# Two hidden-layer products moved, two pieces of an attention product joined, and a shorter spacing of a block inverse in a PE-bound two-layer kernel

## The chip, the cores and the metric

The kernel runs on one core of a Trainium2 chip. TensorE (PE) multiplies, VectorE (DVE) and ScalarE (ACT) move and transform what it leaves in PSUM, GpSimd (POOL) does small elementwise work, and SyncE (SP) issues DMAs. Every engine works through its own list of instructions in order, and semaphores tie the lists together. The metric is the device time of one launch in microseconds, the median of three runs.

## The reference, cut to what matters

Input is `x` of shape (8, 512, 128): eight sequences of 512 tokens. Two layers follow each other, and each multiplies an attention-like term by a gate.

```python
xn = _layernorm(x, axis=-1)
s = _L0_attn_ref(xn, ...)                 # causal softmax attention, 16 heads of 8
g = _silu(_L0_ffn_ref(xn, ...))           # 8 experts, top 2: gelu(x w1 + b1) w2 + b2, weighted by gates
x = x + s * g
xn = _layernorm(x, axis=-1)
s = _L1_attn_ref(xn, ...)                 # h = layernorm; W -= 0.01 * (W k - v) k^T token by token; y = W q
g = _silu(_L1_ffn_ref(xn, weight))        # x @ sign(weight).T
x = x + s * g
```

The expert layer's hidden product is `h = gelu(einsum('bsd,edh->bseh', x, w1) + b1)`. The recurrence of the second layer is computed in four chunks of 128 tokens; each needs the inverse of a unit triangular 128x128 matrix.

## The kernel before, in words

Eight sequences pass through a pipeline. One call of `iteration` is a **round**. In a round four sequences are in work: `second` gets its query and key stacks, `nxt` has its row maxima taken, `cur` its attention, and `prev` its second layer. A full round runs over four groups (0 to 3) of ten units (0 to 9). A unit on TensorE is `s_unit` of `nxt` (L944, L947, read by one VectorE reduction, L1480) and `e_unit` of `cur` (L917, L921, L925, read by one ScalarE exponential, L1265). Each has two PSUM banks, so `s_unit` number u waits for the reduction of u-2 and `e_unit` for the exponential of u-2.

All other work is cut into pieces. The table `PLAN` puts them behind a unit: `(2, 8): ["lev_a5", "k"]` means that behind unit 8 of group 2 come the pieces lev_a5 and k. **Every engine walks the same table**, and runs its own part of a piece at that place of its list. A piece's place thus fixes both when TensorE multiplies and behind which reductions and exponentials VectorE and ScalarE serve it. Group 4 is only the tail of a round: no units, the pieces alone. The pieces the text speaks of:

- `h0` to `h3` (TensorE L865, ScalarE L1244 with the bias): the hidden product of `nxt`, one 128x512 product each into the one bank `ps_a`; `gelu` (L1248) follows on ScalarE, and needs another activation table, as the exponential behind it does again. `gb0` to `gb3` (L872, VectorE L1464) multiply `cur`'s hidden values by the gates; `out` (L879, L881) is the second product, followed by tanh (L1252, ScalarE) and L1469 (VectorE).
- `pv0`, `pv1`, `pv2` (L963): probabilities times values of a group, in three pieces. `yT` is the copy of its bank (L1271 on ScalarE or L1493 on VectorE), `yt` (L973) the transposition behind it, then L1504 and L1507 on VectorE; at the end of a round `x1` (L671, L675 on GpSimd) makes the input of the second layer, whose statistics are L1392 and L1397.
- `lev_a1` to `lev_a6`, `lev_d1` to `lev_d6`: levels of the inverse. Up to level 4 both are 16 products of 32x32 tiles (L1028). ScalarE copies what `lev_a` leaves (L1305), VectorE subtracts what `lev_d` leaves (L1543) and transposes (L1526). The next `lev_a` waits for the subtraction. `low_blocks` (L1564, two VectorE copies) and `turned0`, `turned1` (L1316, two ScalarE copies each) put the squares where `lev_a6` (L1054) reads them; it waits for both.
- `c_u`, `c_y`, `c_r` (L1112; L1122 and L1124; L1101 and L1103): the scan over the four chunks. `c_y` waits for ScalarE's copy of what `c_u` left (L1327), the next `c_u` for VectorE's L1576.
- `xnt`, `q`, `k` (L817, L829) of `second`; ScalarE's cast (L1217) and VectorE's subtraction (L1416) empty the bank behind q and k. `vl0`, `vl1` (L844), `m_rows0`, `m_rows1` (L888, copied by ScalarE L1257) use `ps_a` as well: whoever fills this bank waits until its last user is through.

Of the kernel before, what the change touches and what calls it, by code (L numbers as in the profile page):

```python
# [18 lines left out]
ALU = mybir.AluOpType  # L19
# [5 lines left out]
P = 128  # L25
# [71 lines left out]
PLAN_SECOND = ("load_x", "ln1_stats", "ln1_rstd", "ln1_norm", "xnt", "q", "k", "stacks0", "stacks1")  # L97
PLAN_NEXT = ("rn", "vl0", "vl1", "route", "v_out", "logits", "gates", "gate_norm", "gt", "h0", "h1", "h2", "h3", "gelu", "v", "m_parts0", "m_rows0", "m_parts1")
PLAN_OLDER = ("c_u3", "c_y3", "c_out")
PLAN_CURRENT = ("gb0", "gb1", "gb2", "gb3", "out", "pv0", "pv1", "pv2", "yt", "x1", "m_rows1", "zero_state")  # L100
SEQUENCES = 8


# [39 lines left out]
def iteration(second, nxt, cur, prev, older, plan=PLAN):  # L143

    for step in range(1 + max(at[0] for at in plan)):
        for u in range(UNITS):
            if step < GROUPS:
                yield "unit", (cur, nxt, step, u)
            for name in plan.get((step, u), []):
                if name.startswith("fill"):  # L150
                    yield "fill", (int(name.removeprefix("fill")),)
                    continue
                if name in PLAN_COMMON:
                    yield name, ()
                    continue
                of = second if name in PLAN_SECOND else nxt if name in PLAN_NEXT else \
                    cur if name in PLAN_CURRENT or name.startswith("last:") else older if name in PLAN_OLDER else prev
                name = name.removeprefix("last:").removeprefix("prev:")
                if of is not None:
                    yield name, (of, step) if name in ("pv0", "pv1") else (of, step - 1) if name in ("pv2", "yt") else (of,)  # L160


def schedule():
# [33 lines left out]
def two_layers(nc, x_in, W_dq, W_uq, W_dkv, W_uk, W_uv, W_o, w1_in, b1_in, w2_in, b2_in, cent_in, route_in,  # L197
# [8 lines left out]
    with ExitStack() as ctx:  # L206
        def sb(name, shape, dt=F32):
            return ctx.enter_context(nc.sbuf_tensor(name, shape, dt))
# [518 lines left out]
        def _(pe):  # L727
# [81 lines left out]
            def tok(i):  # L809
                return slice(i * P, (i + 1) * P)  # L810
# [63 lines left out]
            def out_piece(b):  # L874
                a_fill(b, "out")
                pe.wait_ge(S["b2_ready"], PARTS)
                for i in range(NT):
                    for c in range(NC):
                        mm(ps_a[:, tok(i)], hid[:, c, tok(i)], w2s[:, c, :], start=(i == 0 and c == 0), stop=False,  # L879
                           skip_group_check=True)  # L880
                    last = mm(ps_a[:, tok(i)], gT[:, tok(i)], b2s[:, :], start=False, stop=True, skip_group_check=True)  # L881
                last.then_inc(S["a_filled"], 1)

            def m_rows(b, half):
                a_fill(b, f"m_rows{half}")
# [64 lines left out]
                last.then_inc(S["s_filled"], 1)  # L950


            def pv(b, grp, piece):

                if piece == 0:
                    after(pe, S["v_emptied"], b.count(2 * FILLS, 2 * (grp // FILLS)))
                    if grp == 0:
                        pe.wait_ge(S["v_ready"], b.count(FILLS, FILLS))
                pe.wait_ge(S["e_emptied"], b.count(GROUPS * UNITS, UNITS * grp + (4, 8, 10)[piece]))
                for j, u0, at in (((0, 0, 0),), ((1, 4, 0), (3, 4, 384)), ((2, 8, 0),))[piece]:  # L960
                    for hh in range(GH):
                        u, o = (u0 + hh, at) if j != 2 else (u0 + hh // 2, 256 * (hh % 2))
                        last = mm(ps_v[32 * hh:32 * hh + 32, P * j:TOK], vaug[:, j, head_of(grp, hh), :],  # L963
                                  prob[:, u, o:o + TOK - P * j], start=(j == 0 and grp % FILLS == 0),
                                  stop=(j == 2 and grp % FILLS == FILLS - 1), skip_group_check=True)
                last.then_inc(S["pv_used"], 1)

            def yt(b, grp):
                if grp % FILLS < FILLS - 1:
# [145 lines left out]
            def c_y(b, c):  # L1115
# [11 lines left out]
                elif c == NT - 1 - (b.c == SEQS - 1):  # L1127
                    last.then_inc(r.S["c1_filled"], 1)

            pieces = {"xnt": xnt, "q": lambda b: qk(b, 0), "k": lambda b: qk(b, 1), "v": v, "logits": logits, "vl0": lambda b: values_and_logits(b, 0), "vl1": lambda b: values_and_logits(b, 1), "gt": gt,  # L1130
                      "out": out_piece, "m_rows0": lambda b: m_rows(b, 0), "m_rows1": lambda b: m_rows(b, 1), "pv0": lambda b, grp: pv(b, grp, 0), "pv1": lambda b, grp: pv(b, grp, 1), "pv2": lambda b, grp: pv(b, grp, 2), "yt": yt, "c_xn2t": c_xn2t, "c_ht": c_ht, "c_kt": c_kt,
                      "c_qt": c_qt, "c_vk": c_vk, "c_gram": c_gram, "c_ffn": c_ffn}
            for c in range(NC):
                pieces[f"h{c}"] = lambda b, c=c: h(b, c)
# [13 lines left out]
        def _(act):  # L1148
# [92 lines left out]
            def h(b, c):  # L1241
                a_full(b, f"h{c}")
                after(act, S["gelu_ready"], b.count(1, 0))
                af(hid[:, c, :], ps_a[:, :], ACT.Identity, bias=vecT[:, c:c + 1]).then_inc(S["a_emptied"], 1)  # L1244

            def gelu(b):
                act.wait_ge(S["a_emptied"], A_NUMBER[b.c, "h3"] + 1)
                af(hid[:, :, :], hid[:, :, :], ACT.Gelu).then_inc(S["gelu_ready"], 1)  # L1248

            def out_piece(b):  # L1250
                a_full(b, "out")
# [72 lines left out]
            def c_u(b, c):  # L1324
# [3 lines left out]

            pieces = {"xnt": xnt, "q": lambda b: split_hi(b, 0), "k": lambda b: split_hi(b, 1), "v": v, "gates": gates, "gt": gt,
                      "vl0": lambda b: values_and_logits(b, 0), "vl1": lambda b: values_and_logits(b, 1),  # L1330
                      "gelu": gelu, "out": out_piece, "m_rows0": lambda b: m_rows(b, 0), "m_rows1": lambda b: m_rows(b, 1), "pv2": pv, "c_xn2t": c_xn2t, "c_ht": c_ht, "c_kt": c_kt,
                      "c_qt": c_qt, "c_gram": c_gram, "c_ffn": c_ffn}
            for c in range(NC):
                pieces[f"h{c}"] = lambda b, c=c: h(b, c)
# [9 lines left out]
        def _(dve):  # L1344
# [258 lines left out]
            def c_y(b, c):  # L1603
# [9 lines left out]
                else:  # L1613
# [52 lines left out]
```

## Time and profile before

| | |
|---|---|
| median of 3 runs | 616.99 us (615.72 to 617.30) |
| the profiled execution, device time | 615.89 us |
| its span | 614.2 us |
| PE busy | 576.2 us, 94% |
| DVE busy | 391.7 us, 64% |
| ACT busy | 352.7 us, 57% |
| POOL busy | 176.8 us, 29% |
| chain that ended last | PE 80%, DVE 10%, ACT 4% |

Full rounds with four sequences in work start near 185.5, 252.6, 321.2 and 389.9 us in the span; the one from 457.0 us has no `second` any more, and the two from 60.5 and 114.8 us lack the older sequences. All seven use `PLAN`. The last round from 523.0 us has a table of its own, which stays as it is. A time in a row is us from the span's start; PEclk is the granted TensorE clock as a share of full speed.

### The profile page before, as it was taken

The numbers are of one execution on the slowest core, as the hardware profiler recorded it, in microseconds if no ns is written. First come the engines' busy times: TensorE is split into PE (matmuls) and PEld (weight loads), VectorE is DVE, ScalarE is ACT, GpSimd is POOL, SyncE is SP. The second block draws the span as 40 slices with busy tenths as digits, with TensorE's granted clock in tenths as the row PEclk, the third lists the DMA queues.
The fourth block names the chain that finished last, engine by engine and source line by source line (L and its number), as shares of the span: only waits on it lengthen the run. The fifth ranks groups of instructions, "written<-read, shape, count | busy, mean of one in ns | idle before, by whom it ended". The sixth has DMA issues, their size and how long they took to land.

```text
span 614.2 us, 17394 instructions
## 1 busy us (share of the span) xinstructions
PE 576.2 (94%) x7233; PEld 385.2 (63%) x7233; DVE 391.7 (64%) x975; ACT 352.7 (57%) x678; POOL 176.8 (29%) x351
## 2 busy tenths in 40 slices
PE   7789999898998999899998999899998999799897
PEld 3345565476665876677665876678665776555465
DVE  4478775765757776767757676867667675511553
ACT  4421656763666566765666466765675576666231
POOL 7157122411304312431214221532224200311221
PEclk9899999998999999999998999999998999999999
DMA  4766193847134105510253105510262000000001
GB/s 117 151 157 136 25 98 83 160 66 69 53 91 94 45 11 109 120 43 3 62 110 67 44 12 124 103 45 3 72 122 49 22 12 1 26 18 2 3 4 34
DMA packets 58161, 39.41 MB, mean 64 GB/s; under 512 B 17956, under 2 KB 57987, under 8 KB 58083
## 3 DMA queue, kind: packets, MB, share of 16 engines
q1 hardware_dynamic: 58051, 38.29, 31.0%
q8 instruction: 57, 0.93, 0.7%
q14 instruction: 21, 0.17, 0.1%
q10 hardware_dynamic: 32, 0.01, 0.0%
HBM read 24.46 MB, written 9.96 MB: 56 GB/s over the span
## 4 chain that ended last, share of the span: by engine, by line
PE 80%; DVE 10%; ACT 4%; issue 2%; DMA 1%; POOL 1%; SPq 0%; DVEq 0%; POOLq 0%
PE ps_v L963 13%; PE ps_s L944 12%; PE ps_e L925 6%; PE ps_a L879 5%; PE ps_c L1028 4%; PE ps_a L865 4%; PE ps_e L917 3%; PE ps_e L921 3%; DVE cand L1480 3%; PE ps_a L829 3%; PE ps_s L947 3%; PE ps_e L747 3%; PE ps_c L1112 2%; PE ps_c L1010 1%; PE ps_a L844 1%
## 5 line engine op out<-in xcount | busy, mean ns | idle before, releaser
L1480 DVE TENSOR_REDUCE cand<-ps_s 128x4 f32<-128x512 f32 (+1 forms) x320 | 213.5, 686 | 75.9 <-PE ps_s L947 47.5
L1265 ACT ACTIVATE prob<-ps_e 128x512 f32<-128x512 f32 x320 | 187.8, 598 | 88.7 <-PE ps_e L925 52.6
L944 PE MATMUL ps_s<-kst,qst 72*128 72x128 bf16 (+2 forms) x1024 | 126.3, 236 | 15.0 <-DVE cand L1480 11.2
L944 PEld LDWEIGHTS ps_s<-kst,qst 72*128 72x128 bf16 (+1 forms) x1024 | 73.0, 98 | 79.7 <-DVE cand L1480 40.8
L925 PE MATMUL ps_e<-qst,kst 75*128 75x256 bf16 (+3 forms) x416 | 105.4, 284 | 0.0
L963 PE MATMUL ps_v<-prob,vaug 128*32 128x512 f32 (+3 forms) x1024 | 89.5, 451 | 0.0
L917 PE MATMUL ps_e<-identb,negmask 128*128 128x150 bf16 (+3 forms) x320 | 73.2, 229 | 3.2 <-ACT prob L1265 3.0
L921 PE MATMUL ps_e<-qst,kst 128*128 128x128 bf16 x384 | 75.1, 221 | 0.0
L925 PEld LDWEIGHTS ps_e<-qst,kst 75*128 75x128 bf16 x416 | 40.9, 98 | 3.5
L747 PE MATMUL ps_e<-identb 128*128 128x512 bf16 x115 | 40.0, 402 | 1.9 <-POOL identb L521 1.9
L921 PEld LDWEIGHTS ps_e<-qst,kst 128*128 128x128 bf16 x384 | 38.2, 100 | 4.5 <-issue 0.3
L947 PE MATMUL ps_s<-negmask,identb 128*128 128x300 bf16 (+1 forms) x128 | 41.0, 320 | 0.0
L963 PEld LDWEIGHTS ps_v<-prob,vaug 128*32 128x32 f32 x1024 | 24.0, 109 | 25.8 <-issue 20.0
L917 PEld LDWEIGHTS ps_e<-identb,negmask 128*128 128x128 bf16 x320 | 31.4, 98 | 13.9 <-ACT prob L1265 9.4
L1028 PEld LDWEIGHTS ps_c<-second 32*32 32x32 f32 x2072 | 25.2, 107 | 23.3 <-issue 18.2
L650 POOL CAST mparts<-nm 128x32 bf16<-128x32 f32 x16 | 3.3, 209 | 120.7 <-DVE nm L1487 120.7
L1028 PE MATMUL ps_c<-second 32*32 32x32 f32 x2072 | 33.0, 194 | 4.2 <-issue 1.8
L865 PE MATMUL ps_a<-xnT,w1s 128*128 128x512 f32 x64 | 33.6, 605 | 1.3 <-ACT hid L1244 0.8
L879 PE MATMUL ps_a<-w2s,hid 128*128 128x128 f32 x256 | 33.3, 283 | 0.7 <-ACT mrow L1257 0.7
L879 PEld LDWEIGHTS ps_a<-w2s,hid 128*128 128x128 f32 x256 | 31.1, 192 | 1.6 <-ACT mrow L1257 1.0
L1244 ACT ACTIVATE hid<-ps_a,vecT 128x512 f32<-128x512 f32 x32 | 22.0, 687 | 17.1 <-PE ps_a L865 17.1
L696 POOL TENSOR_TENSOR second<-second,second_flat 128x512 f32<-128x512 f32 x7 | 8.9, 1266 | 57.2 <-ACT second_flat L1286 43.4
(344 smaller groups left out, 924.7 us busy)
## 6 DMA issues: line engine op xcount, KB each, us to landing
qst<-q_scratch SPq DMA_DIRECT2D x48, 192.0 KB
kst<-k_scratch SPq DMA_DIRECT2D x48, 192.0 KB
q_scratch<-qparts SPq DMA_DIRECT2D x24, 128.0 KB, 2.3
k_scratch<-kparts SPq DMA_DIRECT2D x24, 128.0 KB, 2.3
x_res<-in_L_attn_x_dram SPq DMA_DIRECT2D x8, 256.0 KB, 4.3
xn<-in_L_attn_x_dram SPq DMA_DIRECT2D x7, 256.0 KB, 3.3
out_dram<-second SPq DMA_DIRECT2D x7, 256.0 KB, 2.5
max_scratch<-mrow SPq DMA_DIRECT2D x16, 96.0 KB, 1.9
```

Of the source, the lines that this page charges most:

```text
L747: mm(ps_e[:, 1, :].rearrange("p (a c) -> p a c", c=P), identb[:, :], bcast(identb[:, :], 1, 4), start=True, stop=True, skip_group_check=True)
L865: mm(ps_a[:, :], w1s[:, 2 * c:2 * c + 2, :].rearrange("p e f -> p (e f)"), xnT[b.parity][:, :], start=True, stop=True)\
L879: mm(ps_a[:, tok(i)], hid[:, c, tok(i)], w2s[:, c, :], start=(i == 0 and c == 0), stop=False, skip_group_check=True)
L917: mm(diag, negmask[:, :], bcast(identb[:, masked:P], 1, len(todo)), start=True, stop=False, skip_group_check=True)
L921: last = mm(ps_e[:, bank, at:at + P], k[:, hd, tok(j)], q[:, hd, tok(j)], start=False, stop=True, skip_group_check=True)
L925: last = mm(ps_e[:, bank, at + own:at + TOK - P * j], k[0:SROWS, hd, tok(j)], q[0:SROWS, hd, P * j + own:TOK], start=False, stop=True, ski ...
L944: last = mm(ps_s[:, bank, w * n:w * (n + 1)], q[0:rows, hd, tok(i)], k[0:rows, hd, keys[0]:keys[1]], start=(n == 0), stop=True, skip_group ...
L947: last = mm(ps_s[:, bank, :].rearrange("p (a c) -> p a c", a=GH)[:, :, masked:P], identb[:, :], bcast(negmask[:, masked:P], 1, GH), start= ...
L963: last = mm(ps_v[32 * hh:32 * hh + 32, P * j:TOK], vaug[:, j, head_of(grp, hh), :], prob[:, u, o:o + TOK - P * j], start=(j == 0 and grp % ...
L1028: last = mm(bank[SQ * col:SQ * col + SQ, SQ * i:SQ * i + SQ], lhsT(row, col, i), rhs[SQ * row:SQ * row + SQ, i, :], start=True, stop=True, ...
L1265: af(prob[:, u, :], ps_e[:, u % 2, :], ACT.Exp).then_inc(S["e_emptied"], 1)
L1480: vec.tensor_reduce(cand[:, i, h0:h0 + FILLS * (len(hds) - 1) + 1:FILLS, S_SLOT[u]], ps_s[:, u % 2, :].rearrange("p (a c) -> p a c", a=len ...
```

## The change

Six things change in the kernel; the arithmetic is the same.

- `h0` and `h1` of `nxt` stand in group 0 behind units 2 and 4, not in group 3. Since `gb` of `cur` still reads its hidden values, `hid` becomes two buffers by parity. `gb0`, `gb1`, `gb2` move back: behind unit 8 of group 0 and units 1 and 2 of group 1.
- `pv1` and `pv2` are one piece `pv12`, at the place of `pv2` (behind unit 2 of the next group).
- The levels stand closer: `lev_a1` stays behind (1, 5), then one step behind nearly each unit; `lev_d6` is at (2, 9) and not at (3, 2).
- `turned0`, `turned1`, `low_blocks` stand at (2, 3), (2, 5), (2, 7) and not at (2, 7), (2, 9), (3, 0).
- The scan fills group 3: `c_u0` at (3, 0), `c_y0` (3, 1), `c_r1` (3, 2) and so on.
- At the end of a round `c_y2` stands ahead of `pv12`, and `c_r3` ahead of `yt`.

```diff
-    (0, 0): ["c_u3"], (0, 1): ["gb0"], (0, 2): ["ln2_stats", "c_y3"], (0, 4): ["ln2_rstd", "hn_norm"],
-    (0, 6): ["pv0"], (0, 7): ["c_ht", "rn", "c_out"], (0, 8): ["gb1"], (0, 9): ["pv1", "c_kt", "c_qt"],
...
-    (2, 9): ["pv1", "lev_d5", "turned1"], (3, 0): ["stacks0", "h0", "low_blocks"], (3, 1): ["lev_a6"], (3, 2): ["h1", "lev_d6", "pv2"], (3, 3): ["c_u0"],
...
+    (0, 0): ["c_u3"], (0, 2): ["ln2_stats", "c_y3", "h0"], (0, 4): ["h1", "ln2_rstd", "hn_norm"],
...
+    (2, 7): ["low_blocks"], (2, 8): ["lev_a6", "k"], (2, 9): ["lev_d6"], (3, 0): ["stacks0", "h2", "c_u0"], (3, 1): ["c_y0"],
...
-        hid = sb("hid", [P, NC, TOK])
+        hid = [sb(f"hid{p}", [P, NC, TOK]) for p in range(2)]
...
-            def pv(b, grp, piece):
+            def pv(b, grp, pieces):
...
-                pe.wait_ge(S["e_emptied"], b.count(GROUPS * UNITS, UNITS * grp + (4, 8, 10)[piece]))
-                for j, u0, at in (((0, 0, 0),), ((1, 4, 0), (3, 4, 384)), ((2, 8, 0),))[piece]:
+                pe.wait_ge(S["e_emptied"], b.count(GROUPS * UNITS, UNITS * grp + (4, 8, 10)[pieces[-1]]))
+                for j, u0, at in [tile for n in pieces for tile in (((0, 0, 0),), ((1, 4, 0), (3, 4, 384)), ((2, 8, 0),))[n]]:
...
-                last.then_inc(S["pv_used"], 1)
+                last.then_inc(S["pv_used"], len(pieces))
...
-                af(hid[:, c, :], ps_a[:, :], ACT.Identity, bias=vecT[:, c:c + 1]).then_inc(S["a_emptied"], 1)
+                af(hid[b.parity][:, c, :], ps_a[:, :], ACT.Identity, bias=vecT[:, c:c + 1]).then_inc(S["a_emptied"], 1)
```

On TensorE at the end of a round and into group 0, before (L872 is gb0, L1124 is c_y3):

```order
L973 MATMUL ps_v<-ident,yT 128x128 x4
L1101 MATMUL ps_c<-state,second_flat 128x128
L1103 MATMUL ps_c<-state,second_flat 128x128
L944 MATMUL ps_s<-kst,qst 128x128 x4
...
L872 MATMUL ps_a<-gT,pick 128x512
L944 MATMUL ps_s<-kst,qst 128x128 x4
...
L1124 MATMUL ps_c<-u_sb,second 128x128
L944 MATMUL ps_s<-kst,qst 128x128 x4
```

and now:

```order
L1101 MATMUL ps_c<-state,second_flat 128x128
L1103 MATMUL ps_c<-state,second_flat 128x128
L973 MATMUL ps_v<-ident,yT 128x128 x4
L944 MATMUL ps_s<-kst,qst 128x128 x4
...
L1124 MATMUL ps_c<-u_sb,second 128x128
L865 MATMUL ps_a<-xnT,w1s 128x512
L944 MATMUL ps_s<-kst,qst 128x128 x4
```

gb0 has left this place, h0 (and behind unit 4 h1) has come in, and the scan's product c_r3 has moved ahead of the transposition.

On VectorE in the second half of group 2, before (xn<-ps_a is q's subtraction, krest<-ps_a that of k):

```order
L1480 TENSOR_REDUCE cand<-ps_s 128x2 x2
L1416 TENSOR_TENSOR xn<-ps_a,qparts 128x512
L1543 TENSOR_TENSOR second<-second,ps_c 128x128
L1526 STREAM_TRANSPOSE second<-second 128x128
L1480 TENSOR_REDUCE cand<-ps_s 128x2 x2
L1416 TENSOR_TENSOR krest<-ps_a,kparts 128x512
```

and now (L1564 is low_blocks):

```order
L1480 TENSOR_REDUCE cand<-ps_s 128x2
L1416 TENSOR_TENSOR xn<-ps_a,qparts 128x512
L1480 TENSOR_REDUCE cand<-ps_s 128x2
L1564 COPY second<-second 32x4x32 x2
L1480 TENSOR_REDUCE cand<-ps_s 128x2
L1416 TENSOR_TENSOR krest<-ps_a,kparts 128x512
```

The two copies that lev_a6 waits for now stand behind q's subtraction and one reduction. On TensorE the same place reads, now (L829 w_q is q, L1054 lev_a6):

```order
L829 MATMUL ps_a<-xnT,w_q 128x512
L944 MATMUL ps_s<-kst,qst 128x256 x2
...
L944 MATMUL ps_s<-kst,qst 128x256 x2
...
L1054 MATMUL ps_c<-second 64x64 x4
L829 MATMUL ps_a<-xnT,w_k 128x512
```

Only two units lie between q and lev_a6.

## Rows read from the trace of the kernel before

**Rows 1.** Two full rounds: stretch, length, busy PE PEld DVE ACT POOL, PEclk, DMA, GB/s
```profile
252.60:321.20 68.60, 66.59 (x900) 46.86 (x898) 47.91 (x121) 43.17 (x83) 20.02 (x36) 0.98 0.29 63
389.90:457.00 67.10, 65.10 (x900) 46.43 (x898) 47.78 (x121) 43.14 (x83) 20.00 (x36) 1.00 0.29 65
```
**Rows 2.** The same view, where the clock is down, and ahead of it
```profile
255.57:258.98 3.41, 1.73 (x23) 1.28 (x23) 3.38 (x13) 1.80 (x4) 1.65 (x4) 1.00 0.91 179
258.98:262.39 3.41, 3.41 (x20) 1.20 (x18) 2.39 (x7) 1.19 (x2) 2.51 (x4) 0.50 0.17 41
463.78:467.19 3.41, 3.41 (x19) 1.26 (x18) 2.08 (x7) 1.16 (x2) 2.21 (x3) 0.50 0.04 9
```
**Rows 3.** Timeline from yt to unit 5: start, us, engine, line [idle before <-releaser]
```profile
388.92 0.66 PE L973 MATMUL ps_v<-ident,yT 128*128 128x128 f32 x4 [0.17 <-DVE yT L1493]
391.86 1.27 POOL L675 TENSOR_TENSOR x<-x_res,att 128x512 f32<-128x512 f32 x1
393.37 0.86 DVE L1392 BATCH_NORM_STATS2 stats<-x 128x6 f32<-128x128 f32 x4
395.13 1.28 DVE L1480 TENSOR_REDUCE cand<-ps_s 128x4 f32<-128x512 f32 x2
395.88 0.39 PE L944 MATMUL ps_s<-kst,qst 72*128 72x256 bf16 x2 [1.68 <-DVE cand L1480]
```
**Rows 4.** Timeline of TensorE: pv1, pv2, and both in one
```profile
341.54 0.64 PE L963 MATMUL ps_v<-prob,vaug 128*32 128x256 f32 x8
342.11 0.40 PE L944 MATMUL ps_s<-kst,qst 128*128 128x128 bf16 x4
...
370.05 1.07 PE L963 MATMUL ps_v<-prob,vaug 128*32 128x384 f32 x16
371.05 0.59 PE L1028 MATMUL ps_c<-second 32*32 32x32 f32 x24
...
386.61 1.50 PE L963 MATMUL ps_v<-prob,vaug 128*32 128x384 f32 x24
388.04 0.49 PE L1122 MATMUL ps_c<-u_sb,vk 128*128 128x128 f32 x2
```
**Rows 5.** Timeline around q, and the two copies of low_blocks later
```profile
366.44 0.45 PE L1028 MATMUL ps_c<-second 32*32 32x32 f32 x32
366.82 0.39 PE L944 MATMUL ps_s<-kst,qst 72*128 72x256 bf16 x2
367.16 0.69 DVE L1416 TENSOR_TENSOR xn<-ps_a,qparts 128x512 f32<-128x512 f32 x1 [1.90 <-ACT qparts L1217]
367.35 0.38 PE L944 MATMUL ps_s<-kst,qst 72*128 72x256 bf16 x2
368.32 1.25 DVE L1480 TENSOR_REDUCE cand<-ps_s 128x2 f32<-128x512 f32 x2
373.22 0.45 DVE L1564 COPY second<-second 32x128 f32<-32x128 f32 x2
```
**Rows 6.** Timeline behind h0
```profile
372.20 1.02 PE L865 MATMUL ps_a<-xnT,w1s 128*128 128x512 f32 x2
373.06 0.38 PE L944 MATMUL ps_s<-kst,qst 128*128 128x128 bf16 x4
373.26 0.69 ACT L1244 ACTIVATE hid<-ps_a,vecT 128x512 f32<-128x512 f32 x1 [0.27 <-PE ps_a L865]
```
**Rows 7.** Timeline behind out
```profile
352.50 0.38 PE L944 MATMUL ps_s<-kst,qst 72*128 72x256 bf16 x2
353.33 0.69 DVE L1469 SCALAR_TENSOR_TENSOR gate_out<-tG,ps_a 128x512 f32<-128x512 f32 x1 [3.16 <-ACT tG L1252]
```
**Rows 8.** Groups of ACT by line: busy us, mean ns of one | idle before
```profile
L1257 ACT COPY mrow<-ps_a 96x512 bf16<-96x512 bf16 x16 | 9.2, 577 | 2.4 <-PE ps_a L888 1.9
L1316 ACT COPY second<-second 32x128 f32<-32x128 f32 x28 | 8.2, 294 | 1.9 <-DVE second L1526 1.4
L1327 ACT COPY u_sb<-ps_c 128x128 f32<-128x128 f32 x28 | 7.3, 262 | 7.9 <-PE ps_c L1112 7.7
```

More of the change, by code:

```diff
@@ L60 @@
 PLAN = {
[9 rows of a table removed]
+    (0, 0): ["c_u3"], (0, 2): ["ln2_stats", "c_y3", "h0"], (0, 4): ["h1", "ln2_rstd", "hn_norm"],
+    (0, 6): ["pv0"], (0, 7): ["c_ht", "rn", "c_out"], (0, 8): ["gb0"], (0, 9): ["c_kt", "c_qt"],
[7 rows of a table added]
 }
@@ L99 @@
 PLAN_OLDER = ("c_u3", "c_y3", "c_out")
-PLAN_CURRENT = ("gb0", "gb1", "gb2", "gb3", "out", "pv0", "pv1", "pv2", "yt", "x1", "m_rows1", "zero_state")
+PLAN_CURRENT = ("gb0", "gb1", "gb2", "gb3", "out", "pv0", "pv1", "pv2", "pv12", "yt", "x1", "m_rows1", "zero_state")
 SEQUENCES = 8
@@ L159, in iteration @@
                 if of is not None:
-                    yield name, (of, step) if name in ("pv0", "pv1") else (of, step - 1) if name in ("pv2", "yt") else (of,)
+                    yield name, (of, step) if name in ("pv0", "pv1") else (of, step - 1) if name in ("pv2", "pv12", "yt") else (of,)
 def schedule():
@@ L878, in out_piece @@
                     for c in range(NC):
-                        mm(ps_a[:, tok(i)], hid[:, c, tok(i)], w2s[:, c, :], start=(i == 0 and c == 0), stop=False,
+                        mm(ps_a[:, tok(i)], hid[b.parity][:, c, tok(i)], w2s[:, c, :], start=(i == 0 and c == 0), stop=False,
                            skip_group_check=True)
@@ L950, in s_unit @@
                 last.then_inc(S["s_filled"], 1)
-            def pv(b, grp, piece):
-                if piece == 0:
+            def pv(b, grp, pieces):
+                if 0 in pieces:
                     after(pe, S["v_emptied"], b.count(2 * FILLS, 2 * (grp // FILLS)))
@@ L1130, in _ @@
             pieces = {"xnt": xnt, "q": lambda b: qk(b, 0), "k": lambda b: qk(b, 1), "v": v, "logits": logits, "vl0": lambda b: values_and_logits(b, 0), "vl1": lambda b: values_and_logits(b, 1), "gt": gt,
-                      "out": out_piece, "m_rows0": lambda b: m_rows(b, 0), "m_rows1": lambda b: m_rows(b, 1), "pv0": lambda b, grp: pv(b, grp, 0), "pv1": lambda b, grp: pv(b, grp, 1), "pv2": lambda b, grp: pv(b, grp, 2), "yt": yt, "c_xn2t": c_xn2t, "c_ht": c_ht, "c_kt": c_kt,
+                      "out": out_piece, "m_rows0": lambda b: m_rows(b, 0), "m_rows1": lambda b: m_rows(b, 1), "pv0": lambda b, grp: pv(b, grp, (0,)), "pv1": lambda b, grp: pv(b, grp, (1,)), "pv2": lambda b, grp: pv(b, grp, (2,)), "pv12": lambda b, grp: pv(b, grp, (1, 2)), "yt": yt, "c_xn2t": c_xn2t, "c_ht": c_ht, "c_kt": c_kt,
                       "c_qt": c_qt, "c_vk": c_vk, "c_gram": c_gram, "c_ffn": c_ffn}
@@ L1243, in h @@
                 after(act, S["gelu_ready"], b.count(1, 0))
-                af(hid[:, c, :], ps_a[:, :], ACT.Identity, bias=vecT[:, c:c + 1]).then_inc(S["a_emptied"], 1)
+                af(hid[b.parity][:, c, :], ps_a[:, :], ACT.Identity, bias=vecT[:, c:c + 1]).then_inc(S["a_emptied"], 1)
             def gelu(b):
                 act.wait_ge(S["a_emptied"], A_NUMBER[b.c, "h3"] + 1)
-                af(hid[:, :, :], hid[:, :, :], ACT.Gelu).then_inc(S["gelu_ready"], 1)
+                af(hid[b.parity][:, :, :], hid[b.parity][:, :, :], ACT.Gelu).then_inc(S["gelu_ready"], 1)
             def out_piece(b):
@@ L1330, in _ @@
                       "vl0": lambda b: values_and_logits(b, 0), "vl1": lambda b: values_and_logits(b, 1),
-                      "gelu": gelu, "out": out_piece, "m_rows0": lambda b: m_rows(b, 0), "m_rows1": lambda b: m_rows(b, 1), "pv2": pv, "c_xn2t": c_xn2t, "c_ht": c_ht, "c_kt": c_kt,
+                      "gelu": gelu, "out": out_piece, "m_rows0": lambda b: m_rows(b, 0), "m_rows1": lambda b: m_rows(b, 1), "pv2": pv, "pv12": pv, "c_xn2t": c_xn2t, "c_ht": c_ht, "c_kt": c_kt,
                       "c_qt": c_qt, "c_gram": c_gram, "c_ffn": c_ffn}
@@ L1463, in gb @@
                 dve.wait_ge(S["gelu_ready"], b.count(1, 1))
-                vec.tensor_tensor(hid[:, c, :], hid[:, c, :], ps_a[:, :], ALU.mult).then_inc(S["a_emptied"], 1)
+                vec.tensor_tensor(hid[b.parity][:, c, :], hid[b.parity][:, c, :], ps_a[:, :], ALU.mult).then_inc(S["a_emptied"], 1)
             def out_piece(b):
@@ L1621, in _ @@
                       "q": lambda b: split_rest(b, 0), "k": lambda b: split_rest(b, 1), "logits": logits, "route": logits, "gates": gates, "gate_norm": gate_norm,
-                      "out": out_piece, "m_parts0": lambda b: m_parts(b, 0), "m_parts1": lambda b: m_parts(b, 1), "pv2": pv, "yt": yt, "c_vk": c_vk, "c_gram": c_gram, "c_ffn": c_ffn, "x1": x1_piece, "early_out": early_out}
+                      "out": out_piece, "m_parts0": lambda b: m_parts(b, 0), "m_parts1": lambda b: m_parts(b, 1), "pv2": pv, "pv12": pv, "yt": yt, "c_vk": c_vk, "c_gram": c_gram, "c_ffn": c_ffn, "x1": x1_piece, "early_out": early_out}
             for c in range(NC):
```

12 rows, old and new, of the table PLAN are left out of this document.

## The prediction

> **What bounds the kernel now.** I read the busy time by stretches first. A full round takes 67.1 us where the clock stays up, and PE is busy for 65.1 of them; VectorE reaches 47.8 and ScalarE 43.1 [rows 1]. So PE's list sets the time: every wait on PE counts in full, and work that moves along it counts only by the waits it fills or makes. Second, the timeline around each start of a round. PE stands for 1.68 us before the `s_unit` of unit 5 in group 0, for VectorE's reduction of unit 3 [rows 3]; so it does in each of five rounds. Third, the clock. One full round takes 68.6 us, not 67.1 [rows 1], with the same count of matmuls. In it the clock is at half (1.2 GHz) for 3.41 us, right behind a stretch in which PE was busy for 1.73 of 3.41 us, the one with the wait [rows 2]. Of the five rounds of [rows 3]'s kind three have this fall (first and last in [rows 2]), the two others not, with the same wait. A fall costs 68.6 - 67.1 = 1.5 us.
>
> **Part 1: h0, h1 in group 0.** What ends the 1.68 us wait is a chain that starts with yt at 388.92: two VectorE pieces, two GpSimd products (x1 ends at 391.86 + 1.27 = 393.13), the statistics from 393.37, a sum, and the reduction of unit 3 (the first of the two from 395.13, so to 395.77); PE goes on at 395.88 [rows 3]. That is 6.96 us from yt. In the new order VectorE has no gb0 in the way (0.69, as any pass over a 128x512 bank, L1469 in [rows 7]), but x1 is hardly earlier than VectorE came anyway (393.13 against 393.37), so the chain still takes 6.8. PE's own work over the same stretch was 6.96 less its waits: 1.68, 0.2 for the exponential behind the activation table, 0.2 for c_u3, so about 4.8. Now c_r3 (0.45) and gb0 (0.22) leave it and h0 and h1 come in, 373.06 - 372.20 = 0.86 each [rows 6]: 4.8 - 0.67 + 1.72 = 5.85. Waits fall from 2.1 to 0.95 us, split into two of half a microsecond. Gain 1.2 us a round. c_r3 gains nothing by itself: it fills the wait for yT that c_y2 filled (PE L973 still waited 0.17 there, [rows 3]).
>
> **Part 2: one piece for two.** pv1 takes 371.05 - 370.05 = 1.00 us of PE's list, pv2 342.11 - 341.54 = 0.57; both in one take 388.04 - 386.61 = 1.43 [rows 4]. So a join is worth 0.14. It happens in groups 0 to 2 (behind group 3 they already ran as one): 0.42 a round, and about 0.1 for one fewer change from wide products to 32-wide ones. 0.5.
>
> **Part 3: the spacing.** PE's work is the same; what counts is whether VectorE and ScalarE, which walk the same table, are through. A unit is 367.35 - 366.82 = 0.53 us of PE [rows 5], with the wider mask product of units 0 to 3 and some of the later ones 0.6.
> - `lev_a6` (largest). q ends at 366.3 (the next piece starts at 366.44); VectorE's subtraction for q runs 367.16 to 367.85, since ScalarE casts first [rows 5]. Behind it now stand one reduction (1.25 / 2 = 0.63) and the two copies of low_blocks (0.45) [rows 5]: 367.8 + 0.6 + 0.45 = 368.8. PE gets there two units behind q, at 366.3 + 0.53 + 0.6 = 367.5. Wait 1.3 us, where none of this kind was. Queued behind lev_a6 on PE are k, and through k the stacks of the next sequence; these had microseconds to spare.
> - `xnt`: waits for ScalarE's copy of m_rows0 (0.58), ahead of which turned0 (2 x 0.29) now stands [rows 8] and, with it, the copy of lev_a5. 0.4.
> - `vl0`: gb2 is one unit ahead of it, and VectorE's product is through 0.42 + 0.69 after gb2 starts (the pass is that of L1469, [rows 7]); PE arrives after 0.22 + 0.6. 0.3.
> - `lev_a3`: lev_d2's subtraction stands behind L1469, which ends at 354.02, 1.5 us after out [rows 7], and one reduction and itself (0.6 + 0.3); PE arrives 2.05 behind out. 0.3.
> - `c_y0`, `c_y1`: each is one unit behind c_u, whose copy (0.26, [rows 8]) stands behind h2's or h3's bias pass, which starts 0.2 after PE's next piece and takes 0.69 [rows 6]: ready after 1.13, PE arrives after 0.84 or 0.80. 0.6 for both.
> - `c_y2` 0.1 and `pv12` 0.3 at the end of a round: pv1 used to run there while the last exponential went on; pv12 needs that one first.
> - `lev_d1` 0.2, behind the transposition that follows gb3 on VectorE.
>
> Together 3.5 us a round. Three small waits of before go (c_y1, c_r1, lev_a5: 0.3). From both sides: the hand-over between engines reads as 0.1 to 0.2 us in these rows, so each of the nine waits may be 0.1 us off: 2.6 to 4.4 a round, 614.5 to 623.5 in the end. I take the middle, which the hand-over behind h0 (373.26 - 373.06 = 0.2, [rows 6]) and that of PE to VectorE's chain (395.88 - 395.77 = 0.1, [rows 3]) give.
>
> **Sum.** A full round: -1.2 - 0.5 - 0.3 + 3.5 = +1.5 us. Five rounds have all this: +7.5. In the round without `second` there is no q and no xnt, so 1.7 less: about 0. The first one has no inverse: joins and h0 against the later pv12, about 0. The clock: with no wait near 1.68 left at the round's start, the three falls go, -4.6. The new 1.3 us wait is shorter than those ahead of any fall, and I cost it no clock. Net +2.9 on 615.89. The median of the runs is 1.1 above that execution, less than one clock fall; since the new kernel has fewer places for falls I add only a little of it. **619.0 us.**
>
> **Rivals.**
> *Faster, 611 us (609 to 614).* The steps cost nothing much: VectorE and ScalarE catch up, and the waits of ScalarE's kind (xnt, c_y0, c_y1, pv12, 1.6 a round) vanish, which leaves 619 - 8 = 611. For it: ScalarE is busy for 43 of 67 us [rows 1]. Against: each wait above is a fixed chain behind PE's own product, not a matter of load.
> *Clock stays as it is, 623.6 us.* The fill is right but the falls have another cause, or the wait at lev_a6 takes them over: 619.0 + 4.6. For it: a fall came in only three of five rounds with the same wait [rows 2]. Against: in these five rounds it never came anywhere else. The Trainium skill (TensorE: Matmul & The Clock Gate, section "HAM oscillation") names as the cause idle gaps longer than any in these rounds; by it the 1.68 us wait costs no clock and this rival would hold. The trace disagrees as far as it goes, the clock being down right behind that wait.
> *No change, 617 us.* The lev_a6 wait is half of mine, as k, which waits on the same subtraction, loses its own wait in turn: 5 x 0.4 less.
> *Slower than all this:* if lev_a6 also held the clock down in every second round and each small wait were 0.1 longer, 625.
>
> **How the numbers follow.** What a measurement of this kernel can tell from no change is 0.3%, 1.85 us: faster is under 615.1, slower over 618.8. The forecast has 0.55 (own range 617 to 622), the faster rival 0.2, the kept clock 0.1, no change 0.15. Half of the forecast's chance and more lies above 618.8, with the kept clock 0.49; the faster rival and a bit make 0.21; 0.30 stays within. Range 612 to 623.5.
>
> **What the new profile would show.** The wait before L944 of unit 5 in group 0 near 0.5 us with L865 ahead of it, and PEclk at 1.00 in the full rounds. L963 in runs of 24 of 1.43 us. A wait of 1.3 us before L1054 on VectorE's L1564, the largest of the round; waits near 0.3 before L1122, before L817 on L1257, before L844 on L1464. Rounds of 68.6 us without a fall, against 67.1. I am wrong if rounds are under 67.1: then the wait at L1054 is missing or the chain behind yt is shorter than 6.8.

## The result: 3.1% slower, and the profile after

| | before | after |
|---|---|---|
| median of 4 runs each | 617.14 us (615.72 to 621.37) | 636.44 us (633.61 to 642.59) |
| the profiled execution, device time | 615.89 us | 638.92 us |
| its span, mean granted clock | 614.2 us, 0.986 | 637.2 us, 0.973 |

The ratio is 1.0314, with a 95% interval from 1.0252 to 1.0375. The forecast was 619.0 us (612 to 623.5): the direction was right, the size was not. Here and below the ratios are taken without the slow executions of a kernel (over 1.5% above its fastest, among them one of e5 of 1835.67 us and one of e6 of 900.86 us), while the medians are over all.

The same four rounds as around [rows 1], now with the changed kernel (stretch, length, busy PE PEld DVE ACT POOL, PEclk, DMA, GB/s):

```profile
192.20:266.30 74.10, 70.00 (x900) 49.84 (x899) 49.11 (x120) 43.07 (x83) 20.06 (x36) 0.93 0.25 58
266.30:339.50 73.20, 68.89 (x901) 48.69 (x900) 49.12 (x120) 43.11 (x83) 20.06 (x36) 0.95 0.25 60
339.50:409.40 69.90, 65.61 (x900) 46.80 (x898) 48.93 (x120) 42.92 (x83) 20.05 (x36) 1.00 0.27 63
409.40:481.00 71.60, 67.30 (x900) 47.74 (x899) 49.18 (x120) 43.09 (x83) 20.03 (x36) 0.98 0.27 61
```

One round has no clock fall: 69.9 us against 67.1, with the same number of matmuls and 0.5 us more of busy PE. The other 2.3 us of the 2.8 are waits. The other three rounds are 1.7, 3.3 and 4.2 us longer than that one, in step with their clock. VectorE is busy 1.1 us longer in a round, for the same work; that is the first sign of what follows.

Where PE waits (engine, line waited for, us in total, times, longest us):

```profile
PE ps_c L1054 <- issue: 12.3, 6, 2.4
PE ps_e L917 <- ACT prob L1265: 3.3, 6, 1.4
PE ps_s L944 <- DVE cand L1480: 3.3, 7, 1.1
PE ps_c L1028 <- issue: 2.9, 1, 2.9
PE ps_c L1028 <- DVE second L1543: 2.6, 6, 1.6
...
PE ps_c L1122 <- ACT u_sb L1327: 1.9, 10, 0.2
PE ps_v L973 <- DVE yT L1493: 1.9, 7, 0.8
```

The wait at `lev_a6` (L1054) is the largest: 2.4 us in each of five rounds (and 0.4 in a sixth), not the 1.3 forecast. It is listed under "issue", since the profile shows no releaser for it. The timeline in the clear round shows who was late (start, us, engine, line, [idle before <-releaser]):

```profile
386.77 0.69 DVE L1416 TENSOR_TENSOR xn<-ps_a,qparts 128x512 f32<-128x512 f32 x1 [1.81 <-ACT qparts L1217]
...
387.38 0.68 DVE L1480 TENSOR_REDUCE cand<-ps_s 128x2 f32<-128x512 f32 x1
387.53 0.61 POOL L616 CAST qparts<-xn 128x512 bf16<-128x512 f32 x1 [8.56 <-DVE xn L1416]
387.98 1.47 DVE L1564 COPY second<-second 32x128 f32<-32x128 f32 x2
388.22 1.15 POOL L618 TENSOR_TENSOR qparts<-xn,qparts 128x512 bf16<-128x512 f32 x1
...
389.55 0.65 PE L1054 MATMUL ps_c<-second 64*64 64x64 f32 x8 [2.40 <-issue]
```

The two copies of `low_blocks` (L1564) take 1.47 us, where [rows 5] has 0.45. They end at 389.45, and PE starts 0.1 later. GpSimd's second piece for q runs beside them, from 388.22 to 389.37 (L618; it is a subtraction, the expectations below call it a product). The durations of one copy, after and then before (ns min/median/max, first and last start):

```profile
L1564 DVE COPY second<-second x14: 203/234/1206, 167.6 to 608.3; 32x128 f32<-32x128 f32 x14
```
```profile
L1564 DVE COPY second<-second x14: 203/217/498, 168.6 to 585.2; 32x128 f32<-32x128 f32 x14
```

The second copy is the long one: 1205 or 1206 ns in all five rounds, where it takes 217 with GpSimd idle. It starts 0.03 us behind GpSimd's subtraction (1.15 us) and ends 0.08 behind that one's end. The first copy overlaps the end of GpSimd's cast (L616), ends 0.07 us behind it, and takes 233 to 235 ns, not 203 to 205. By this the copy is not slowed: it stands still until GpSimd is through. The Trainium skill (SBUF — State Buffer, section "SBUF: two separate sides") states this: VectorE in some of its modes and GpSimd share one pair of ports, and the pair "is an **exclusive lock**, not a bandwidth split"; who comes second waits for the whole instruction of the other. The trace agrees for this copy, with 1206 ns against 217.

This could be read in the trace of the kernel before. There the same subtraction stands at the very place where the copies were going to be put, and late in the span a copy already meets another GpSimd piece (L686):

```profile
367.92 0.61 POOL L616 CAST qparts<-xn 128x512 bf16<-128x512 f32 x1 [6.66 <-DVE xn L1416]
368.61 1.15 POOL L618 TENSOR_TENSOR qparts<-xn,qparts 128x512 bf16<-128x512 f32 x1
...
584.11 0.99 POOL L686 TENSOR_TENSOR qst<-qst,up_sq 128x384 f32<-128x384 f32 x1
584.67 0.75 DVE L1564 COPY second<-second 32x128 f32<-32x128 f32 x2
```

That pair takes 0.75 us and not 0.45; its first copy is the 498 ns above, and ends 0.07 us behind L686. Not all of VectorE's work is held so: the two reductions of [rows 5] from 368.32 (1.25 us for the two, as usual) run beside the subtraction from 368.61.

The clock, ahead of and behind this wait in the first and in the last of the three full rounds with a fall:

```profile
238.38:241.79 3.41, 1.52 (x15) 0.95 (x12) 2.23 (x4) 1.63 (x3) 1.43 (x2) 1.00 0.15 41
241.79:245.21 3.42, 2.90 (x11) 1.60 (x12) 1.11 (x2) 0.37 (x1) 0.33 (x1) 0.50 0.29 77
245.21:248.62 3.41, 3.41 (x27) 3.00 (x26) 2.08 (x4) 1.18 (x2) 1.74 (x2) 0.50 0.14 38
248.62:252.03 3.41, 3.41 (x15) 2.19 (x14) 0.80 (x2) 1.44 (x3) 0.02 (x1) 0.50 0.30 79
...
456.83:460.25 3.42, 1.02 (x15) 0.81 (x13) 3.26 (x5) 0.97 (x3) 1.76 (x2) 1.00 0.29 77
460.25:463.66 3.41, 3.41 (x17) 2.00 (x18) 0.92 (x2) 1.48 (x3) 0.17 (x1) 0.50 0.16 43
```

The clock is at half (1.2 GHz) for 10.2 us in the first of them (it falls 0.5 us before the wait ends there, and 0.5 to 1.0 us after its end in the others), 6.8 in the second and 3.4 in the last; in the round of the first inverse it is so for 6.8 us from 170.1, behind the wait that ends at 169.1. That is four of five. [Rows 2] showed the same at the start of a round, never for more than 3.4 us. These old falls are gone: no full round now falls at its start.

### The profile page after: what moved, and what is told of

The parts are those of the page before. It is cut to its first block, busy times and chain, and to the rows that moved or that the text cites. A ratio compares the mean times of both kernels' runs of the same rounds, so it can differ in the third digit from the quotient of the medians.

```text
span 637.2 us, 17394 instructions
## 1 busy us (share of the span) xinstructions
PE 586.7 (92%) x7233; PEld 393.8 (62%) x7233; DVE 398.1 (62%) x975; ACT 352.2 (55%) x678; POOL 177.1 (28%) x351
## 4 chain that ended last, share of the span: by engine, by line
PE 74%; DVE 7%; issue 7%; ACT 6%; POOL 4%; DMA 1%; SPq 0%; POOLq 0%; DVEq 0%
PE ps_v L963 12%; PE ps_s L944 11%; PE ps_e L925 6%; PE ps_a L879 5%; PE ps_c L1028 4%; PE ps_a L829 3%; PE ps_a L865 3%; PE ps_e L917 3%; PE ps_e L747 3%; PE ps_e L921 3%; PE ps_s L947 2%; PE ps_a L844 2%; PE ps_c L1122 2%; PE ps_c L1010 1%; DVE cand L1480 1%
## 5 line engine op out<-in xcount | busy, mean ns | idle before, releaser
L944 PEld LDWEIGHTS ps_s<-kst,qst 72*128 72x128 bf16 (+1 forms) x1024 | 75.9, 100 | 65.2 <-DVE cand L1480 29.7
L963 PE MATMUL ps_v<-prob,vaug 128*32 128x512 f32 (+3 forms) x1024 | 82.8, 439 | 0.7 <-ACT prob L1265 0.7
L1028 PEld LDWEIGHTS ps_c<-second 32*32 32x32 f32 x2072 | 25.3, 107 | 26.1 <-issue 18.4
L963 PEld LDWEIGHTS ps_v<-prob,vaug 128*32 128x32 f32 x1024 | 25.2, 109 | 24.8 <-issue 21.0
L1028 PE MATMUL ps_c<-second 32*32 32x32 f32 x2072 | 33.0, 194 | 6.5 <-issue 2.9
L865 PE MATMUL ps_a<-xnT,w1s 128*128 128x512 f32 x64 | 36.1, 648 | 1.4 <-ACT hid L1244 0.8
L1464 DVE TENSOR_TENSOR hid<-hid,ps_a 128x512 f32<-128x512 f32 x32 | 21.8, 681 | 10.1 <-PE ps_a L872 10.0
```

What stands on the lines that cost most here:

```text
L865: mm(ps_a[:, :], w1s[:, 2 * c:2 * c + 2, :].rearrange("p e f -> p (e f)"), xnT[b.parity][:, :], start=True, stop=True)\
L944: last = mm(ps_s[:, bank, w * n:w * (n + 1)], q[0:rows, hd, tok(i)], k[0:rows, hd, keys[0]:keys[1]], start=(n == 0), stop=True, skip_group ...
L1028: last = mm(bank[SQ * col:SQ * col + SQ, SQ * i:SQ * i + SQ], lhsT(row, col, i), rhs[SQ * row:SQ * row + SQ, i, :], start=True, stop=True, ...
```

## The experiments

Theory: the loss is the wait before `lev_a6`, and that wait has two parts that the forecast did not price, VectorE's copy standing behind GpSimd's subtraction (1.1 us) and the clock behind the wait. Rivals: GpSimd's piece is a bystander; the clock falls for some other reason; or the loss lies in the many small waits or in the two other parts of the change. Each table line below is one kernel. "Before" ran beside them on the same chip; its median was 617.14 for the result, 618.24 for e1 to e4, and 616.14 for e5 to e8, so between these three groups the ratio is what can be compared.

| kernel | median us | ratio to before [95%] |
|---|---|---|
| changed kernel | 636.44 | 1.031 [1.025, 1.038] |
| e1, copies before q | 613.38 | 0.996 [0.991, 1.000] |
| e2, GpSimd held back | 632.19 | 1.024 [1.017, 1.031] |
| e3, wait filled with products | 628.72 | 1.016 [1.011, 1.021] |
| e4, parts 1 and 2 without part 3 | 608.01 | 0.983 [0.979, 0.987] |
| e5, part 1 alone | 606.65 | 0.987 [0.983, 0.992] |
| e6, part 2 alone | 620.99 | 1.010 [1.006, 1.014] |
| e7, part 3 alone | 646.35 | 1.053 [1.045, 1.061] |
| e8, e4 with three waits filled | 601.11 | 0.979 [0.972, 0.986] |

**e1.** The changed kernel with one piece moved two units up:

```diff
-    (2, 5): ["xnt", "lev_d5", "turned1"], ... (2, 7): ["low_blocks"], (2, 8): ["lev_a6", "k"],
+    (2, 5): ["xnt", "lev_d5", "low_blocks", "turned1"], ... (2, 8): ["lev_a6", "k"],
```

> The changed kernel (profiled 638.9 us), with one piece moved: low_blocks, VectorE's two copies L1564, stands behind lev_d5 at (2, 5) and no longer behind q's subtraction at (2, 7). Theory 1 (lev_a6 waits for these copies, which stand late and collide there with GpSimd's product L618; the wait of 2.4 us brings the clock down): the wait before L1054 goes to under 0.2 us in all five full rounds, no clock falls near it, full rounds near 69.9 - 2.4 = 67.5 us; time 638.9 - 12.6 (falls) - 5 x 2.4 = 614, range 611 to 618. Rival (the profile puts the wait down to issue: PE's own instructions come late there): the wait before L1054 stays near 2.4 us and so does the time, 633 to 642.

Measured: 613.38 us, as expected, and 23 less than the changed kernel (22 by the ratios). The wait before L1054 is gone from the list of waits, the copies are back at 214/216/509 ns, and no full round has a clock fall. A full round is 67.6 us:

```profile
318.60:386.20 67.60, 65.71 (x901) 46.93 (x900) 47.90 (x120) 43.07 (x83) 20.05 (x36) 1.00 0.29 64
```

VectorE is at 47.90 us again. So the whole loss hangs on this one place: 69.9 - 67.6 = 2.3 us in each round, and the falls. The small waits of the new spacing are all still there and are not the cause of the loss. They do cost something: 67.6 us is 0.5 more than the clear round of before, though parts 1 and 2 are in.

**e2.** GpSimd's two pieces for q (cast and subtraction) now start behind the copies, the table is that of the changed kernel (the line numbers of its rows are two higher):

```diff
                 pool.wait_ge(S["a_emptied"], A_NUMBER[b.c, ("q", "k")[n]] + 1)
+                if n == 0 and b.c >= 3:
+                    pool.wait_ge(S["blocks_ready"], 2 * (b.c - 3) + 2)
```

> The changed kernel, order unchanged, but GpSimd's work on q (L616, L618) waits until VectorE's two copies L1564 are through. Theory 1 says that the second copy takes 1.2 us instead of 0.24 since it runs while GpSimd's L618 does: both copies then take 0.24, the wait before L1054 is 1.4 us as first forecast, and the clock falls less or not at all: full rounds near 68.9, time 619 to 623. Rival a (the copy is slow for another reason, such as its place or a VectorE wait): it stays at 1.2 us and the time at 633 to 642. Rival b (the port costs what I say, but a wait of 1.4 us still brings the clock down): time 624 to 632 with PEclk at 0.5 behind L1054.

Measured: 632.19 us. The same place of its timeline, and its largest waits:

```profile
377.90 0.45 DVE L1566 COPY second<-second 32x128 f32<-32x128 f32 x2
...
378.45 0.65 PE L1056 MATMUL ps_c<-second 64*64 64x64 f32 x8 [1.38 <-issue]
378.49 0.61 POOL L618 CAST qparts<-xn 128x512 bf16<-128x512 f32 x1 [9.59 <-DVE second L1566]
```
```profile
PE ps_c L1056 <- issue: 7.2, 6, 1.4
```

Nothing changed for VectorE but the moment at which GpSimd works, and the copies take 0.45 us again: GpSimd's subtraction was what held them. The wait is 1.4 us, the forecast's 1.3 within a tenth. The time, however, is not the 619 to 623 that I expected, but just above the 624 to 632 of rival b. It fell by 4.2 us, near the five times 1.0 that the waits give but not clear of the spread (the intervals of the two ratios overlap), and it is still 18.8 above e1. Of these, 7.2 are the waits. The clock is at half for 6.8 us behind two of them, at 379.7 and at 451.4; at 3.3 us each, as between the rounds of 73.2 and 69.9 above, that is 6.6. Another 3.4 come from falls at places that have nothing to do with this wait (one in the first round, and the one at 151.0, which lasts 6.8 us where e1 has 3.4). The remaining 1.6 are within the spread of its runs. So a wait of 1.4 us brought the clock down too, in two of five rounds, and the forecast would have been too low even with its own wait.

**e3.** The wait is as it was, but PE multiplies in it: ten 128x512 products into a free bank ahead of `lev_a6`, with results that nothing reads.

```diff
-    (2, 7): ["low_blocks"], (2, 8): ["lev_a6", "k"],
+    (2, 7): ["low_blocks"], (2, 8): ["warm", "lev_a6", "k"],
```

> The changed kernel, and ahead of lev_a6 TensorE runs ten extra 128x512 bf16 products (of the identity, into a bank that is free there; their result is overwritten). They take about 0.22 us each, 2.2 us, and fit into the wait. Theory 1: the wait for L1564 remains but PE is busy, so the clock stays up; full rounds 69.9 to 70.2 us, time 638.9 - 12.6 = 626, range 624 to 629. Rival (the clock falls for another reason, the order of the work behind q or the draw of this stretch): falls of 3.4 to 10 us remain behind L1054, time 633 to 642, or more by what does not fit.

Measured: 628.72 us, as expected. In its timeline the copies (L1571 there) still take 1.47 us, and PE's own wait is down to 0.24:

```profile
377.92 1.47 DVE L1571 COPY second<-second 32x128 f32<-32x128 f32 x2
...
379.49 0.65 PE L1054 MATMUL ps_c<-second 64*64 64x64 f32 x8 [0.24 <-issue]
```

Its clock is 0.992 against 0.973, with no fall in the full rounds behind `lev_a6`. The delay itself is unchanged: all four full rounds are 70.0 us, as long (within 0.1) as the clear one of the changed kernel. So 636.44 - 628.72 = 7.7 us is what the clock alone cost, in medians (9 by the ratios, whose intervals do not overlap). To e1 15.3 us are left. Of these, five times 2.4 = 12.0 are the stretch before `lev_a6`, now filled instead of empty; for the rest the trace has two falls elsewhere (3.4 us more at 147.7 than e1, and 3.4 at 540.2), 1.7 each. So the loss has two parts, some 8 to 9 us of clock and 12 of waiting, and no third of their size.

**e4.** The table of before with h0 and h1 in group 0, gb0 to gb2 moved back, and the joined pieces; levels, `turned`, `low_blocks`, the scan and the order at the end of a round as they were.

```diff
-    (2, 9): ["pv1", "lev_d5", "turned1"], (3, 0): ["stacks0", "h0", "low_blocks"], (3, 1): ["lev_a6"], (3, 2): ["h1", "lev_d6", "pv2"],
+    (2, 9): ["lev_d5", "turned1"], (3, 0): ["stacks0", "h2", "low_blocks"], (3, 1): ["lev_a6"], (3, 2): ["lev_d6", "pv12"],
```

> The changed kernel with the levels, turned0 and 1, low_blocks and the scan back at their places of before: h0 and h1 in group 0 with the two hidden buffers, and pv12, remain. My sum for these parts: -1.2 and -0.5 us a round, +0.3 for vl0 behind gb2, +0.3 for pv12 at the end of a round that must wait for the last exponential, and no clock falls at the start of a round (-4.6): 615.9 - 6 x 1.1 - 4.6 = 604.7, range 601 to 609. Rival (the h move or the joined piece themselves make the kernel slow): 616 or more.

Measured: 608.01 us, 1.7% under before. The start of a round has no fall any more. Its full rounds, however, are 67.2 us, no shorter than the clear ones of before, and its list of waits says why:

```profile
317.20:384.40 67.20, 65.01 (x901) 46.62 (x901) 48.09 (x121) 43.10 (x83) 20.09 (x36) 1.00 0.29 65
```
```profile
PE ps_c L1054 <- issue: 4.7, 5, 1.0
PE ps_v L963 <- ACT prob L1265: 3.2, 7, 0.7
```

pv1 used to stand between k and `lev_a6` and took 1.0 us. Without it PE gets to `lev_a6` that much earlier, and VectorE does not: the join turns work into a wait. At the end of a round the joined piece waits for the last exponential, which pv1 used to cover. I had put `lev_a6` into group 2 for the changed kernel, where this could not be seen. The 608.01 lies in the range that I gave (601 to 609), but not for my reasons: the 1.1 us a round did not come. The time came from the three old falls and from the round of the first inverse, 68.1 us here and 70.6 before, where a fall and a stall inside a level (L1028) are missing in this execution.

**e5.** e4 without the join: pv1 and pv2 apart, at the places of before.

> The order of before with h0 and h1 in group 0 and gb0 to gb2 moved back for them, and nothing else. Theory: the move takes most of the 1.68 us wait at the start of a round and with it the clock falls, and since pv1 stays between k and lev_a6 as before, the 1.0 us wait that the joined order has before lev_a6 does not arise, nor the 0.4 us at the end of a round. Full rounds 66.1 us where the joined one had 67.15: 602.5 us (600 to 605). Rival (my forecast's reading, by which a join is worth 0.5 us a round): without the joins 3 us more than with them, 611 us.

Measured: 606.65 us. A full round is 66.3 us, as expected, 0.9 less than in e4, and the waits before L1054 are gone:

```profile
318.10:384.40 66.30, 65.39 (x902) 46.50 (x900) 47.99 (x121) 43.00 (x83) 20.06 (x36) 1.00 0.28 65
```

The median is 4 us above what I expected. Its profiled execution gives back 3.4 us in the round from 114.0 (71.5 us, where e4 had 68.1), in which the first inverse is computed; the clock falls there twice. Which of e4 and e5 is faster as a whole the runs do not decide, since their ratios' intervals overlap. What is shown is the 0.9 us in the full rounds.

**e6 and e9.** The table of before with the joined pieces alone.

```diff
-    (0, 9): ["pv1", "c_kt", "c_qt"], ... (1, 2): ["c_gram", "pv2"],
+    (0, 9): ["c_kt", "c_qt"], ... (1, 2): ["c_gram", "pv12"],
```

> The order of before with pv1 and pv2 in one piece in all four groups, and nothing else. Theory: the piece itself saves 0.14 us three times, but its millisecond place matters more: without pv1 behind unit 9 of group 2, PE reaches lev_a6 1.0 us earlier and waits there for VectorE, and at the end of a round it waits 0.4 us for the last exponential. Full round +1.0 us, and the waits and falls at the round's start stay: 622 us (619 to 626). Rival (forecast): a join saves 0.5 us a round, 614 us.

> The kernel of e6 once more, for one profile, since the profiled execution of e6 ran at half the clock almost throughout. Theory: a wait of 1.0 us before lev_a6 (L1054) in five rounds, with the 1.68 us wait before L944 at the start of the rounds still there, and 0.5 us before the joined piece at the end of a round; clear rounds of 68.1 us. Rival: no wait at L1054 and clear rounds of 66.6 us.

Measured: 620.99 us, 1% slower than before: my forecast's reading (614) falls, and the theory's 622 stands. The profile is that of e9, one further execution of the same kernel, of 615.18 us. Its full round and its waits:

```profile
322.10:390.10 68.00, 64.59 (x901) 46.59 (x899) 47.91 (x121) 43.15 (x83) 20.10 (x36) 1.00 0.28 65
```
```profile
PE ps_s L944 <- DVE cand L1480: 11.2, 8, 1.7
PE ps_c L1054 <- issue: 4.7, 5, 0.9
PE ps_v L963 <- ACT prob L1265: 3.2, 7, 0.7
```

PE is busy for 0.5 us less than in [rows 1] and the round is 0.9 longer. Note also that the 1.7 us wait at the start of a round is there in each of them, and the clock stays up in the full ones. In this execution the wait of [rows 3] cost no clock at all in these rounds; in that of before it did in three of five. (One early round of e9 does have a fall, at 118.7, behind a wait of 1.48 us at the same place.)

**e7.** The changed kernel with everything but the spacing put back.

```diff
-    (0, 2): ["ln2_stats", "c_y3", "h0"], (0, 4): ["h1", "ln2_rstd", "hn_norm"],
+    (0, 1): ["gb0"], (0, 2): ["ln2_stats", "c_y3"], (0, 4): ["ln2_rstd", "hn_norm"],
```

> The changed kernel with its closer levels and scan, but with h0, h1, gb0 to gb2 and the pieces of probabilities times values at the places of before. Theory: it carries both kinds of clock falls, those at the round's start behind the 1.68 us wait and those behind lev_a6's 2.4 us wait, and is the slowest of all: 640 us (634 to 645). Rival (the parts of the change hurt together, not this one alone): 625 us or less.

Measured: 646.35 us, the slowest. Both waits stand in its list, and its clock is 0.966. As in the changed kernel, the clock falls at four of the five waits before `lev_a6`; at the five waits of 1.6 us at the round's start it falls twice:

```profile
PE ps_c L1054 <- issue: 12.3, 6, 2.4
PE ps_s L944 <- DVE cand L1480: 10.8, 9, 1.6
```

So part 3 by itself is worth +5.3%, and parts 1 and 2 together -1.7% (e4). Their sum, 3.6%, agrees with the 3.1% of all three within the intervals, so no large dependence shows between them. (The sixth item of the change, the order at the end of a round, is in neither e4 nor e7 and was not run alone.) I had expected 6 us less for e7; the trace shows two reasons, a longer wait for xnt's bank (L817, up to 0.6 us where 0.4 was forecast) and one stall of 4.8 us inside a level (L1028) in the round of the first inverse, 2.9 in the changed kernel's.

**e8.** e4 with its three waits filled by work that is there anyway: the joined piece of group 2 ahead of `lev_a6`, gb2 ahead of the joined piece of group 0, and pv1 and pv2 apart at the end of a round.

```diff
-    (1, 2): ["c_gram", "pv12", "gb2"], ... (3, 1): ["lev_a6"], (3, 2): ["lev_d6", "pv12"],
-    (3, 9): ["c_u2"], ... (4, 1): ["pv12", "c_y2"],
+    (1, 2): ["c_gram", "gb2", "pv12"], ... (3, 1): ["pv12", "lev_a6"], (3, 2): ["lev_d6"],
+    (3, 9): ["c_u2", "pv1"], ... (4, 1): ["pv2", "c_y2"],
```

> e4's order with three places mended: the joined piece of group 2 stands ahead of lev_a6 instead of behind lev_d6 (fills 0.95 us), gb2 ahead of the joined piece of group 0 instead of behind it (0.33 us), and at the end of a round pv1 and pv2 are apart as before (0.47 us). Theory: these are waits of PE in the clear and the clock stays up, so full rounds come to 65.4 us: 599.5 us (597 to 602). Rival: VectorE is the next limit there and takes the gain back as waits elsewhere, 604 us or more.

Measured: 601.11 us, as expected: 2.1% under before and, by the ratios, 5.1% under the changed kernel; the fastest here.

```profile
315.30:380.60 65.30, 64.64 (x902) 46.55 (x900) 48.10 (x121) 42.76 (x83) 20.05 (x36) 1.00 0.29 67
```

A full round has 0.7 us left in which PE is not busy; in [rows 1] it was 2.0. VectorE did not become the limit.

## Why the prediction was wrong, by its own steps

Lengths of a piece are taken from one start to the next on PE, in the clear round after (339.5 to 409.4) and before (389.9 to 457.0).

- **Part 1, h0 and h1: right.** Group 0 up to the end of unit 5 takes 6.85 us, before 6.61, though about 1.8 us of h0 and h1 came in and 0.22 of gb0 left: 1.3 us of waits gone, forecast 1.2. The wait at unit 5 is 0.38, with L865 ahead of it. The falls at the round's start are gone. In e5 it is worth 1.3% by itself.
- **Part 2, the join: right here.** L963 in runs of 24 takes 1.43 us, three times 0.14 less. At the round's end, c_y2, the joined piece and the waits cost 0.28 together, forecast 0.4. That the same join costs a round 0.9 us in the old spacing (e9) was outside my sum.
- **Part 3, the small waits: right.** Unit to unit: xnt 0.4 (forecast 0.4), vl0 0.4 (0.3), lev_a3 0.27 (0.3), c_y0 and c_y1 0.63 (0.6), lev_d1 0.16 (0.2).
- **Part 3, `lev_a6`: wrong in size.** The term was "the two copies of low_blocks (0.45)": they took 1.47 beside GpSimd's subtraction. From the start of the last unit ahead of lev_a6 to lev_a6 itself it is now 3.08 us, 2.40 of them the wait. I took the 0.45 from a row in which GpSimd was idle, and moved the copies to right behind the subtraction whose result GpSimd takes up 0.1 us later. The wait came out at 2.4 us where I had 1.3, in each of five rounds. The bounds of my own sum (2.6 to 4.4) did not hold it, because I gave every wait the same error of 0.1.
- **The clock: wrong.** "I cost it no clock." I argued from length: 1.3 was shorter than the 1.68 ahead of any fall. With 2.4 us the clock fell in four of five rounds, and with 1.4 (e2) in two of five.

The sum, in the profiled executions, is 638.92 - 615.89 = 23.0 us where I had +7.5 and -4.6. The clear round is +2.8, so 14.0 for the five rounds with the whole change, 6.5 more than forecast, of which 5.5 are `lev_a6`. The old falls went as forecast, -4.6. New falls at `lev_a6` cost 4.2 + 3.3 + 1.7 = 9.2 in the full rounds. The round of the first inverse is 5.8 longer than before, 2.8 of it as in a clear one; of the other 3.0, 1.1 are the stall inside a level (L1028 under "issue": 2.9 us, before 1.8), whose cause is open, and 1.9 are left for its new fall. That makes 11.1 for the clock, forecast 0. The round from 60.4 and the one from 481.0, forecast at about 0, add 1.0 and 0.7 (without its old fall). The sum is 14.0 + 11.1 + 1.1 - 4.6 + 1.7 = 23.3. So of the 20 us that I missed, 11 are clock and 5.5 the copies.

Of the rivals, the one with lev_a6 taking over the falls named the mechanism, but priced it at one 1.5 us fall for each old one; these falls last up to 10.2 us, not 3.4. (The faster rival's "1.6 a round" has a slip: its four terms, 0.4 + 0.6 for the two scan waits + 0.3, make 1.3.) The Trainium skill's rule that I weighed there (TensorE: Matmul & The Clock Gate, section "HAM oscillation") speaks of longer idle gaps than any in these rounds. The runs do not bear out that only those matter: filling the gap (e3) or removing it (e1) kept the clock up in the full rounds.

What stays open is when a given wait brings the clock down. The 1.68 us wait did so in three of five rounds before and in none of the full rounds of e9; the 2.4 us wait left one round untouched; 0.95 us never did in e4 or e9.

## What to carry to other kernels

Before you move a short VectorE copy that another engine waits for, look in the timeline at what GpSimd does at the new place, not the old one: a duration read where GpSimd is idle says nothing of it. Price a new wait on TensorE with the clock as well, from zero upwards: here, at `lev_a6`, waits of 0.95 us never brought a fall and waits of 1.4 us did in two of five rounds, and the falls behind the new wait were up to three times as long as any in the profile before. And when work is joined or saved, ask which wait it used to cover: here a join that took 0.14 us less each time cost a round 0.9 us where it stood behind the wait.

## What the runs showed of the hardware

A VectorE copy of 32x128 elements took 1206 ns instead of 217 when GpSimd's 128x512 subtraction started 0.03 us ahead of it, and was through 0.08 us behind that subtraction's end. GpSimd's own piece took 1152 ns, and 1154 before. VectorE's reductions of a PSUM bank beside the same piece took their usual time (1.25 us for two). The clock's falls varied between executions of one kernel: of the changed kernel's four, the mean clock was 0.963 to 0.981 and the time 642.59 to 633.61 us, the lower clock with the longer time. They lasted 3.4, 6.8 or 10.2 us.
